# A GRU and RNN pipeline on one core: GpSimd's softmax weight and x2 move two steps later, behind r's products

## What is computed

```python
x = x + rnn(x, cond)            # h = tanh(h @ Wh + x_t @ Wx + b), in sequence over 2048 steps
w = softmax over the batch of (cond . x_t) / sqrt(512)
x = x + x * w
x = x + tanh(x @ W_ih.T + cond @ W_hh.T + b_ih + b_hh)
x = x + gru(x, cond)            # z, r = sigmoid(...); c = tanh(x_t @ Wh + (r*h) @ Wh' + b)
                                # h = (1-z)*h + z*c; every 4th step h = tanh(h @ Wp + bp)
```

## Time and profile before

| | |
|---|---|
| median of 3 runs | 7811.31 us (7810.34 to 7812.74) |
| profiled execution, its time | 7813.76 us |
| its span | 7812.0 us |
| TensorE matmul / weight load busy | 7654.8 us (98%) / 7258.6 us (93%) |
| VectorE, ScalarE, GpSimd busy | 5742.1 (74%), 4569.4 (58%), 1778.9 us (23%) |
| mean granted clock of TensorE | 0.994 |

### The profile page before, as it was taken

The page is one execution under the profiler, slowest core; times in us unless marked ns, Lnnn a source line. Parts: engine busy times, 40 slices in busy tenths (PEclk is TensorE's granted clock), DMA queues, the critical chain, the costliest instruction groups (busy, mean ns, idle before and its releaser), DMA issues.

```text
span 7812.0 us, 1077031 instructions
## 1 busy us (share of the span) xinstructions
PE 7654.8 (98%) x489016; PEld 7258.6 (93%) x489016; DVE 5742.1 (74%) x31681; ACT 4569.4 (58%) x27004; POOL 1778.9 (23%) x7950
## 2 busy tenths in 40 slices
PE   6999999999999999999999999999999999999998
PEld 5999999999999999999999999999999999999997
DVE  4777777777777777777777777777777777777776
ACT  2555556555555555555555555555565555555554
POOL 2222222222222222222222222222222222222221
PEclk7999999999999999999999999999999999999999
DMA  2000000000000000000000000000000000000000
GB/s 73 12 11 12 13 12 11 12 13 12 11 13 13 11 11 13 12 11 12 13 12 11 12 13 12 11 12 13 12 11 12 13 12 11 13 13 11 11 13 8
DMA packets 153794, 105.06 MB, mean 13 GB/s; under 512 B 19072, under 2 KB 152576, under 8 KB 152576
## 3 DMA queue, kind: packets, MB, share of 16 engines
q1 hardware_dynamic: 153728, 104.22, 4.3%
HBM read 62.20 MB, written 41.94 MB: 13 GB/s over the span
## 4 chain that ended last, share of the span: by engine, by line
PE 97%; DVE 1%; issue 1%; ACT 0%; POOL 0%; DMA 0%; SPq 0%; POOLq 0%; DVEq 0%; ACTq 0%
PE ps_r L499 24%; PE ps_c L499 24%; PE ps_l L488 18%; PE ps_z L488 18%; PE ps_mid L466 7%; PE ps_p L477 6%; DVE p_T L718 1%; ACT h_odd L972 0%; DVE ps_c L722 0%; DVE l_T L718 0%; POOL l_state L397 0%; POOL l_state L401 0%; DMA rnn_h<-w_rnn_h 0%; ACT l_state L892 0%; DVE l_pre L768 0%
## 5 line engine op out<-in xcount | busy, mean ns | idle before, releaser
L499 PE MATMUL ps_c<-c_h,rh 128*2 128x64 f32 x131072 | 2244.1, 219 | 12.4 <-issue 11.2
L499 PEld LDWEIGHTS ps_c<-c_h,rh 128*2 128x2 f32 x131072 | 1901.3, 84 | 36.7 <-issue 13.2
L488 PE MATMUL ps_l<-rnn_h_parts,l_state 128*6 128x128 bf16 x98304 | 1790.2, 220 | 51.9 <-POOL l_state L401 47.2
L943 ACT ACTIVATE r_tanh<-ps_r 128x4 f32<-128x4 f32 x4096 | 711.9, 174 | 1651.2 <-DVE ps_r L722 1580.6
L488 PEld LDWEIGHTS ps_l<-rnn_h_parts,l_state 128*6 128x6 bf16 x98304 | 1517.7, 86 | 64.2 <-ACT ps_l L859 50.9
L722 DVE STREAM_TRANSPOSE ps_r<-ps_r 128x64 f32<-128x64 f32 x4096 | 1087.8, 266 | 485.4 <-PE ps_r L499 381.8
L499 PE MATMUL ps_r<-r_h,h_odd 128*2 128x64 f32 x65536 | 1134.0, 219 | 60.8 <-ACT h_odd L972 54.6
L722 DVE STREAM_TRANSPOSE ps_c<-ps_c 128x64 f32<-128x64 f32 x4096 | 1073.1, 262 | 111.2 <-PE ps_c L499 13.7
L499 PEld LDWEIGHTS ps_r<-r_h,h_odd 128*2 128x2 f32 x65536 | 949.2, 85 | 198.1 <-ACT h_odd L972 95.5
L499 PE MATMUL ps_r<-r_h,h_even 128*2 128x64 f32 x65536 | 1103.7, 219 | 12.4 <-DVE h_even L840 7.8
L397 POOL TENSOR_TENSOR l_state<-l_state 128x8 f32<-128x8 f32 x2048 | 415.2, 203 | 3048.7 <-ACT l_state L892 2722.0
(11 more groups left out here) (106 smaller groups left out, 10116.8 us busy)
## 6 DMA issues: line engine op xcount, KB each, us to landing
gates_spill<-gates_rows SPq DMA_DIRECT2D x128, 192.0 KB, 1.9
gates_seeds<-gates_spill SPq DMA_DIRECT2D x768, 16.0 KB
x_next<-xT SPq DMA_DIRECT2D x128, 64.0 KB, 1.8
x_mid<-xT SPq DMA_DIRECT2D x128, 64.0 KB, 1.8
rnn_spill<-rnn_rows SPq DMA_DIRECT2D x128, 64.0 KB, 1.6
rnn_seeds<-rnn_spill SPq DMA_DIRECT2D x512, 16.0 KB
gates_seeds<-gates_spill SPq DMA_DIRECT2D x512, 8.0 KB
gates_seeds<-gates_spill SPq DMA_DIRECT2D x256, 32.0 KB
```

The source lines that it names most:

```text
L488: last = nc.tensor.matmul(psum[QUAD * j:QUAD * j + PARTS * B, 0:P], state_parts(k), w_parts[:, k, j, q, :], start=False, stop=(k == KT - 1 ...
L499: last = nc.tensor.matmul(pair[QUAD * j:QUAD * j + B, n, at:at + W], stationary(k), w[:, k, P * j + W * n:P * j + W * (n + 1)], start=Fals ...
L943: nc.scalar.activation(r_tanh[:, k, :], r_T[n][:, :, 0:B], ACT.Tanh, scale=0.5).then_inc(r_tanh_done[n], 1)
```

## The change

GpSimd's pieces of the middle for steps 4 to 7 are gathered in `softmax_pair(i, u)`, called after `output` and before `split`. `shifted` stays in step 4 and `denom` in step 5. `weight` and `weight1` move from step 5 to step 6, and `x2` to step 7, in two parts of two feature tiles each. `beside_transpose` makes GpSimd wait for r_product[n] of the step that is running: weight for the low half, weight1 for the high half, the first part of x2 for the low half and the second for the high half.

```diff
+            def beside_transpose(i, u, n):
+                if LAG <= i if isinstance(i, int) else True:
+                    after(pool, r_product[n], STEPS * (i - LAG) + u + 1)
+
+            def softmax_pair(i, u):
+                if u == 4:
+                    pool.wait_ge(top_done, i)
+                    tt(by_step(shifted[:, :]), by_step(logit[:, :]), top[:, :].unsqueeze(2).to_broadcast([P, STEPS, B]),
+                       ALU.subtract).then_inc(shifted_done, 1)
+                if u == 5:
+                    pool.wait_ge(expd_done, i)
+                    tt(denom[:, :], by_step(expd[:, :])[:, :, 0], by_step(expd[:, :])[:, :, 1], ALU.add).then_inc(denom_done, 1)
+                if u == 6:
+                    pool.wait_ge(inv_done, i)
+                    beside_transpose(i, u, 0)
+                    tt(by_step(weight[:, :]), by_step(expd[:, :]), inv[:, :].unsqueeze(2).to_broadcast([P, STEPS, B]),
+                       ALU.mult).then_inc(weight_done, 1)
+                    pool.wait_ge(weight_done, i)
+                    beside_transpose(i, u, 1)
+                    tt(weight1[:, :], weight[:, :], ones[:, :], ALU.add).then_inc(weight1_done, 1)
+                if u == 7:
+                    pool.wait_ge(weight1_done, i)
+                    for n, k in enumerate((slice(0, KH), slice(KH, KT))):
+                        beside_transpose(i, u, n)
+                        last = tt(x2[:, k, :], x1[:, k, :], weight1[:, :].unsqueeze(1).to_broadcast([P, KH, ROWS]), ALU.mult)
+                    last.then_inc(x2_done, 1)
...
                     if gru and u > 0:
                         output(i, u - 1)
-                    if mid and u == 5:
-                        pool.wait_ge(expd_done, i)
-                        tt(denom ...)
+                    if mid and 4 <= u < 8:
+                        softmax_pair(i, u)
                     if rnn_behind(i, u):
                         split(i, u - 1)
...
-                    if mid and u == 4:
-                        pool.wait_ge(top_done, i)
-                        tt(shifted ...)
-                    if mid and u == 5:
-                        pool.wait_ge(inv_done, i)
-                        tt(weight ...)
-                        pool.wait_ge(weight_done, i)
-                        tt(weight1 ...)
-                        pool.wait_ge(weight1_done, i)
-                        tt(x2[:, :, :], x1[:, :, :], weight1[:, :].unsqueeze(1).to_broadcast([P, KT, ROWS]), ALU.mult).then_inc(x2_done, 1)
```

More of the change, by code:

```diff
@@ L413, in iteration @@
                         output(i, u - 1)
-                    if mid and u == 5:
-                        pool.wait_ge(expd_done, i)
-                        tt(denom[:, :], by_step(expd[:, :])[:, :, 0], by_step(expd[:, :])[:, :, 1], ALU.add).then_inc(denom_done, 1)
+                    if mid and 4 <= u < 8:
+                        softmax_pair(i, u)
                     if rnn_behind(i, u):
@@ L434, in iteration @@
                         tt(qx_sum[:, :], qx_half[:, 0, :], qx_half[:, 1, :], ALU.add).then_inc(qx_sum_done, 1)
-                    if mid and u == 4:
-                        pool.wait_ge(top_done, i)
-                        tt(by_step(shifted[:, :]), by_step(logit[:, :]), top[:, :].unsqueeze(2).to_broadcast([P, STEPS, B]),
-                           ALU.subtract).then_inc(shifted_done, 1)
-                    if mid and u == 5:
-                        pool.wait_ge(inv_done, i)
-                        tt(by_step(weight[:, :]), by_step(expd[:, :]), inv[:, :].unsqueeze(2).to_broadcast([P, STEPS, B]),
-                           ALU.mult).then_inc(weight_done, 1)
-                        pool.wait_ge(weight_done, i)
-                        tt(weight1[:, :], weight[:, :], ones[:, :], ALU.add).then_inc(weight1_done, 1)
-                        pool.wait_ge(weight1_done, i)
-                        tt(x2[:, :, :], x1[:, :, :], weight1[:, :].unsqueeze(1).to_broadcast([P, KT, ROWS]), ALU.mult).then_inc(x2_done, 1)
                     if mid and u == 9:
```

## The result

The changed kernel takes 7883.5 us (median of 4 runs, 7880.6 to 7886.6) against 7811.1 us before. The ratio is 1.0092, 95% interval 1.0080 to 1.0104: slower by 72 us. The forecast was 7,901 us, with a range of 7,879 to 7,931.

What follows compares the result with a forecast made beforehand. TensorE's program order bounds the kernel: 0.94 us a chunk lost to the late split, 0.04 to rh's delay, 0.27 gained, so 0.71 times 127 = +90 us on 7811.3, giving 7,901 us, range 7,879 to 7,931.

Steps and rivals of the forecast that it cites:

- What bounds the kernel: TensorE in program order holds 97% of the span; GpSimd matters only by late handovers and by disturbing VectorE.
- Part 3: Step 4: `shifted`, now ahead of the split, makes it wait for top; TensorE loses 0.94 us a chunk, 119 us.
- Nothing later absorbs it: After step 4's pause, each later stage is TensorE's own time or a chain from its products, so the loss stays.
- Part 1 and 2: Steps 5 to 7: weight, weight1, x2 leaving step 5 gain 0.27 us a chunk; beside rh they cost 0.04.
- Scans of h_odd back to 0.50 us: Sign in step 5: VectorE's two scans of h_odd take 0.50 us, where they took 0.79.
- 0.20 idle gone: Sign in step 5: the 0.20 us that TensorE's ps_r waited for VectorE disappears.
- The sum: Per chunk 0.94 + 0.04 - 0.27 = 0.71 us, times 127 = +90 us, giving 7,901 us.
- the split's lateness is hidden: Rival: step 4's late split doesn't hold TensorE, only the gain shows; 7,782 us; chance 0.04.
- all comes to nothing: Rival: nothing measurable, within 0.2% or 16 us, at a split lateness of 0.11 to 0.35 us; chance 0.03.
- The clock: Rival: TensorE's clock falls in step 4's new pause, costing 2.0 us more a chunk; 8,160 us; chance 0.03.
- rh is blocked for the whole of GpSimd's instruction: Rival, steps 6 and 7: the moved work gives back most of its gain; around 7,925 us; chance 0.10.
- GpSimd's wake-up after r's products: Steps 6 and 7: GpSimd assumed released when VectorE is; shown nowhere, it may be later.

Runs made afterwards that it cites:

- e2: The kernel before with only `shifted` moved ahead of the split in step 4; weight, weight1 and x2 stay in step 5; 7912.5 us, ratio 1.0131.
- e1: The changed kernel with `shifted` put back behind the split in step 4; 7778.3 us, 0.9959 of the kernel before.
- e5: The changed kernel with `shifted` computed a second time, into an unread tile, before the split of step 4; 7908.1 us, ratio 1.0127 to the kernel before.
- e6: The changed kernel with VectorE's `top` of step 4 ahead of z's transpose; 7820.5 us, ratio 1.0015 to the kernel before.
- e10: e1 with x2 in one piece, released by r's high product; 7799.6 us, ratio 0.9985 to the kernel before.
- e4: e1 without the three beside_transpose calls, so no waits on r's products; 7775.3 us, ratio 0.9956 to the kernel before.
- e7: e4 with x2 as one instruction; 7798.7 us, ratio 0.9986 to the kernel before.

## Why the prediction was right, by its steps

The time lies inside the stated range, but near its edge: 7883.5 us is what the forecast gets with all its ends low (7,884), and it is inside by 4.5 us because the range had been widened downwards. No single term was far off; all three erred in the same direction.

**What bounds the kernel** held: TensorE's order, and the waits of TensorE for GpSimd as the place to look. **Part 3**, that `shifted` drags the split behind `top`, was the decisive reading, and it came from the diff against GpSimd's queue in the earlier trace rows, not from what the change is about. e2 shows it alone (+103 us), e1 its absence, e5 and e6 that it scales both ways.

**Its size** was too large: 0.94 us a chunk against 0.83 (step 4 of e2 and of the changed kernel, by the matmul starts; e2's medians give 0.81, its mean chunk 0.84). Two things were off.
- From L401's start to ps_l's first load I took 0.32 us from the earlier trace rows. It is 0.25 here (2018.61 to 2018.86), in all 126 new waits, and in most of the waits before the GRU starts it is 0.32. That row is from another stage, where TensorE's clock stands at 0.53; no run shows whether the clock makes the difference. This is 0.07 us, the larger part.
- I took the pause from ps_l's load before, 4037.72, though its matmuls started at 4037.78, and after a wait there is no such lead. So 0.06 us of my pause was none, and the 0.03 that I let come back for the wait for the scan made up for half of it.

"Nothing later absorbs it" held: by the matmul starts ps_l to ps_r takes 0.67 us after the pause and 0.68 before, and step 5 is as long as ever. The view that the starts of the loads tell best when a product began doesn't hold right behind a wait.

**Part 1 and 2.** The net gain of the moved work was forecast at 0.27 - 0.04 = 0.23 us a chunk; e1 gives 0.25 by its median and 0.26 by its mean chunk. In two parts (matmul starts, medians over 122 chunks): steps 5 and 6 won 0.28, as the reciprocal, for which I had kept 0.02, costs nothing, and rh's delay cost 0.02 in place of 0.04. ps_c's loads did start 0.05 us late, but by the matmul starts it was 0.02. "Scans of h_odd back to 0.50 us" and "0.20 idle gone" came true.

**The sum**: 0.94 + 0.04 - 0.27 = 0.71 was forecast, 0.83 + 0.02 - 0.28 = 0.57 measured, and 127 times that is 72 us. The direction and the mechanism were right. Of the 18 us between 7,901 and 7,883 the pause explains 14 and the other two terms about 4.

**The rivals.** That the split's lateness is hidden, and that all comes to nothing, fell with the waits (31 to 157). The clock didn't fall: the mean granted clock is 0.994 before and after, and in the windows of step 4 with the pause and of step 5 behind it (columns as in the earlier trace rows) it stands at 1.00:

```profile
2015.56:2019.48 3.92, 3.26 (x222) 3.07 (x226) 2.89 (x17) 2.92 (x18) 0.99 (x5) 1.00 0.00 0
2019.48:2022.67 3.19, 3.19 (x240) 3.16 (x228) 2.43 (x14) 1.76 (x12) 0.40 (x2) 1.00 0.00 0
```

That rh is blocked for the whole of GpSimd's instruction fell in this kernel: the second part of x2 ended 0.20 us after rh's usual start, and ps_c was late by 0.05. e10 shows what the rule of the Trainium skill ("SBUF — State Buffer", "Who interferes with whom") gets right: rh can't finish before GpSimd's instruction does. (The page calls the shared ports an exclusive lock, but says "for the whole instruction" only of VectorE's two-port modes; of an instruction with two SBUF inputs, such as rh, it says that it contends.) The rows add a price: as rh's end, not its start, is what waits, 0.33 us of overlap costs 0.18.

What GpSimd's wake-up after r's products takes was open in the forecast. It is 0.05 us behind VectorE's (2026.62 and 2026.67), as I had assumed within that.

## What to carry to other kernels

When a diff gathers pieces of work into one call, write down the in-order queue of that engine before and after, item by item; the piece that nobody meant to move can cost more than the moved ones bring. Ask of each piece ahead of which releases it now stands, and when its own wait ends: `shifted` took 0.25 us, but with its wait it put off the start of the split by 1.2 us (2.68 us behind the step's ps_r instead of 1.48). And take durations for a sum from rows of the same stage. Where a product has waited, compare the starts of its matmuls and not of its loads.

## What the runs showed of the hardware that I hadn't expected

- When TensorE runs on without a wait, a product's weight loads start up to 0.06 us ahead of its matmuls (ps_l 4037.72 and 4037.78); when it has been held, both start together (2018.86 after the pause in step 4, 4025.55 for ps_z in e4). Measured by the loads the held product seems to pass in 0.62 us instead of 0.70 to 0.74 (after a pause of 0.90, 0.39 and 1.10 us in step 4 alike, and after 0.07 and 0.19 in e4 and e7), and the next one seems to be 0.05 late; by the matmuls both take what they always take, 0.67 and 0.89 us.
- When a two-input instruction of VectorE meets a GpSimd instruction that reads SBUF and started first, it ends 0.02 to 0.04 us behind it, whether that one took 0.25, 0.32 or 0.46 us: the first scan 4041.63 after weight1 4041.59 and the second 4042.17 after x2 4042.13, the split of the state 4025.49 after 4025.46 in e4 and 4036.79 after 4036.76 in e7, rh 4040.18 after 4040.16 in e10 (the ends of single instructions of the traces; the rows merge some of them). Its start stands in the rows at the usual time, so part of its work seems to go on meanwhile; the runs don't show which.
